# Delta layer with the value folded into the reduce, one fold on GpSimd and eight taps on TensorE, keys moved from SBUF to SBUF, and full-height chunks in the expert layer

## What is computed

```
h = einsum('bsd,ehd->bseh', xn, w_up);  val, gate = split(h, 2)
h = val * silu(gate)                       # 704 hidden values
y = einsum('bseh,edh->bsed', h, w_down)    # 704 -> 256
```

```
q = silu(x @ Wq);  k = silu(x @ Wk);  k = k * rsqrt(sum(k*k) + 1e-12);  v = x @ Wv
beta = 2*sigmoid(x @ Wbet);  a = sigmoid(x @ Wf)
def step(S, inp):
    qt, kt, vt, at, bt = inp
    Sd = at * S
    u  = vt - einsum('bhk,bhkv->bhv', kt, Sd)
    Sn = Sd + bt * kt[..., None] * u[:, :, None, :]
    o  = einsum('bhk,bhkv->bhv', qt, Sn)
    return Sn, o
o = o * rsqrt(mean(o*o) + 1e-6) * norm_w;  return o @ Wo
```

## Time and profile before

| | us |
|---|---|
| median of 3 runs (lowest, highest) | 1418.88 (1416.88, 1424.58) |
| the profiled execution's own time | 1413.77 |
| its span in the trace | 1412.1 |
| TensorE, busy in the span | 1141.6 (81%) |
| VectorE, busy | 826.9 (59%) |
| ScalarE / GpSimd, busy | 564.8 (40%) / 565.7 (40%) |
| mean granted TensorE clock | 0.915 of full speed |

### The profile page before, as it was taken

How to read it: one execution, slowest core, us unless ns; L and a number is a source line. 1 busy time by engine, 2 the same in 40 slices (tenths; PEclk the granted TensorE clock), 3 DMA queues, 4 the chain that set the end, 5 groups by cost and what they waited for, 6 DMA issues and landing times. The chain is left out here.

```text
span 1412.1 us, 23993 instructions
## 1 busy us (share of the span) xinstructions
PE 1141.6 (81%) x8723; PEld 841.3 (60%) x8723; DVE 826.9 (59%) x1978; ACT 564.8 (40%) x1340; POOL 565.7 (40%) x626
## 2 busy tenths in 40 slices
PE   6999984898999999686667777774699999867854
PEld 4666662787889889532234444433577777645533
DVE  3666666211211211456999999997477777532886
ACT  2544552111111112155565666663234444325544
POOL 0111111232333233243699999995122222120657
PEclk9999995899999999799898999997799999979885
DMA  4111100988888887387000000001100040026601
GB/s 134 43 46 46 35 13 13 355 341 319 308 308 316 302 316 267 98 219 191 0 0 1 0 1 0 1 0 59 28 9 13 9 153 36 2 76 255 205 19 57
DMA packets 83349, 162.19 MB, mean 115 GB/s; under 512 B 44128, under 2 KB 62176, under 8 KB 77216
## 3 DMA queue, kind: packets, MB, share of 16 engines
q1 hardware_dynamic: 55536, 111.23, 23.0%
q0 software_dynamic: 10512, 45.10, 8.7%
q10 hardware_dynamic: 17184, 4.33, 1.4%
HBM read 134.28 MB, written 26.35 MB: 114 GB/s over the span
## 5 line engine op out<-in xcount | busy, mean ns | idle before, releaser
L1419 PE MATMUL banks<-made,ident 128*128 128x512 f32 x256 | 152.3, 680 | 91.2 <-DVE made L1630 90.6
L920 PE MATMUL banks<-rowsT,w_up 128*128 128x128 f32 x1716 | 201.3, 278 | 0.0
L920 PEld LDWEIGHTS banks<-rowsT,w_up 128*128 128x128 f32 x1716 | 198.0, 195 | 0.5 <-issue 0.3
L1682 POOL TENSOR_TENSOR ys<-xT_d,q_by_time 128x1024 f32<-128x1024 f32 x63 | 148.6, 2359 | 19.7 <-ACT xT_d L1502 9.8
L1525 ACT ACTIVATE banks<-banks,rate 128x256 f32<-128x256 f32 x256 | 103.9, 444 | 117.7 <-DVE made L1621 117.7
L1419 PEld LDWEIGHTS banks<-made,ident 128*128 128x128 f32 x256 | 41.5, 203 | 155.5 <-ACT banks L1525 130.3
L1686 POOL TENSOR_TENSOR ys<-ys 128x512 f32<-128x512 f32 x126 | 124.8, 990 | 9.9
L935 PE MATMUL banks<-w_down,hT 128*128 128x256 f32 x468 | 115.1, 388 | 0.6 <-DVE res L1100 0.6
L1090 DVE TENSOR_TENSOR hT<-banks,silu 64x128 f32<-64x128 f32 x39 | 11.0, 282 | 171.4 <-ACT silu L978 171.4
L864 POOL DMA_DIRECT2D w_down<-in_down_w x39 | 22.7, 583 | 199.8 <-PE banks L935 191.2
L935 PEld LDWEIGHTS banks<-w_down,hT 128*128 128x128 f32 x468 | 82.6, 189 | 22.0 <-issue 13.9
(11 more groups left out here) (312 smaller groups left out, 2305.8 us busy)
## 6 DMA issues: line engine op xcount, KB each, us to landing
w_up<-in_up_w SPq DMA_DIRECT2D x39, 1408.0 KB, 6.0
w_down<-in_down_w POOLq DMA_DIRECT2D x39, 768.0 KB, 5.6
inter<-res_x SPq DMA_DIRECT2D x16, 512.0 KB, 3.3
back<-inter SPq DMA_DIRECT2D x15, 512.0 KB, 3.9
patches<-in_patches SPq DMA_DIRECT2D x16, 384.0 KB, 3.3
f<-in_f SPq DMA_DIRECT2D x6, 1024.0 KB, 11.5
ys<-token_rows SPq DMA_DIRECT2D x16, 256.0 KB, 2.9
xn_rows<-xn_all SPq DMA_DIRECT2D x16, 128.0 KB, 1.7
```

What stands on the lines that cost most here:

```text
L920: ins = pe.matmul(out[:, m * P:(m + 1) * P], w[:, c, m * P:(m + 1) * P], x[:, c, :], start=(c == 0), stop=(c == 1))
L1419: pe.matmul(S[(t + 1) % 2][:, halves[h], :, :], ident[:, :], outer[:, halves[h], :, :], start=False, stop=True, skip_group_check=True).the ...
L1682: pool.tensor_tensor(qs[:, :, :, :], Sc[(t + 1) % 2][:, :, :, :], bcast(qt[:, t, :, :], 2, HD), ALU.mult).then_inc(sem("qs_made"), 1)
```

## The change

Four edits.

1. Experts: the sixth product of `down` takes all 128 rows. GpSimd zeroes the lower 64 rows of that chunk in both `hT` buffers once (the weights are padded in DRAM already), and TensorE waits for that once.
2. Recurrence, VectorE: `ka` is made with a minus sign, `prod` has 17 elements a value instead of 16, and the 17th is v. So one reduce of 544 elements gives u, and L1627 goes. The 17th element is written by ScalarE (`place_values`), for token t+1 between the fades and `copy_out`, and it waits for u of token t.
3. Recurrence, GpSimd and TensorE: one fold (16 to 8) instead of two, and eight slices in `sum_folded` instead of four, four of them after each half's `add_outer`.
4. Front: the keys go from `made` to `chain_k` straight, in 16 DMAs a group of 16 x 8 x 64 elements (32 KB); no DRAM. The columns of Wk are reordered for it on the host's side of the weights, so that a piece holds 16 heads x 8 dimensions.

```diff
@@ expert_layer
+        for p in range(2):
+            pool.memset(hT[p][HLAST:P, FULL, :], 0.0).then_inc(sem("h_padded"), 1)
...
             for c in range(HIDC):
-                n = P if c < FULL else HLAST
-                ins = pe.matmul(Y, hT[j % 2][0:n, c, :], w_down[j % DEEP][0:n, c, :], start=(c == 0),
-                                stop=(c == FULL))
+                ins = pe.matmul(Y, hT[j % 2][:, c, :], w_down[j % DEEP][:, c, :], start=(c == 0), stop=(c == FULL))
...
+        pe.wait_ge(sem("h_padded"), 2)
@@ delta_layer, SyncE
         def send_keys(g):
-            store_made(sp, g, 2)
-            store_made(sp, g, 3)
+            for m in (2, 3):
+                sp.wait_ge(sem(f"made{m}"), g + 1)
+                for b in range(8):
+                    lanes, dims = slice(b * HEADS, (b + 1) * HEADS), slice(m % 2 * 8, m % 2 * 8 + 8)
+                    sp.dma_start(k[lanes, g, dims, :], made[m][:, b * TOK:(b + 1) * TOK]
+                                 ).then_inc(sem(f"stored{m}"), 16)
...
-            load_chain(sp, g, "k", k)
@@ TensorE
-        def sum_folded(t):
-            pe.wait_ge(sem("qs_folded"), 2 * t + 2)
-            if t:
-                pe.wait_ge(sem("o_made"), t)
-            for n in range(4):
-                ins = pe.matmul(o_sum, ident[:, :], products[t % 2][:, :, :, n], start=(n == 0), stop=(n == 3))
-            ins.then_inc(sem("o_folded"), 1)
+        def sum_folded(t, h):
+            if h == 0:
+                pe.wait_ge(sem("qs_folded"), t + 1)
+                if t:
+                    pe.wait_ge(sem("o_made"), t)
+            for n in range(FOLDED // 2 * h, FOLDED // 2 * (h + 1)):
+                ins = pe.matmul(o_sum, ident[:, :], products[t % 2][:, :, :, n], start=(n == 0),
+                                stop=(n == FOLDED - 1))
+            if h:
+                ins.then_inc(sem("o_folded"), 1)
...
-            add_outer(t)
-            if t >= 2:
-                sum_folded(t - 2)
+            for h in range(2):
+                add_outer(t, h)
+                if t >= 2:
+                    sum_folded(t - 2, h)
@@ ScalarE
+        def place_values(t, h):
+            return act.copy(prod[:, halves[h], :, HD], v[:, halves[h], :, t])
...
+                if t + 1 < TOK:
+                    act.wait_ge(sem(f"u_made{h}"), t + 1)
+                    ins = place_values(t + 1, h)
                 ins.then_inc(sem(f"faded{h}"), 1)
@@ VectorE
-                dve.tensor_tensor(prod[:, at, :, :], S[t % 2][:, at, :, :], bcast(ka[:, t, at, :], 2, HD),
+                dve.tensor_tensor(prod[:, at, :, 0:HD], S[t % 2][:, at, :, :], bcast(ka[:, t, at, :], 2, HD),
                                   ALU.mult).then_inc(sem(f"prod_made{h}"), 1)
                 dve.wait_ge(sem(f"prod_made{h}"), t + 1)
-                dve.tensor_reduce(read[:, at, :], prod[:, at, :, :], AX.X, ALU.add
-                                  ).then_inc(sem(f"read_made{h}"), 1)
-                dve.wait_ge(sem(f"read_made{h}"), t + 1)
-                dve.tensor_tensor(u[:, at, :], v[:, at, :, now].rearrange("p g d o -> p g (d o)"),
-                                  read[:, at, :], ALU.subtract).then_inc(sem(f"u_made{h}"), 1)
+                dve.tensor_reduce(u[:, at, :], prod[:, at, :, :], AX.X, ALU.add).then_inc(sem(f"u_made{h}"), 1)
@@ GpSimd
-            for i, n in enumerate((8, 4)):
-                pool.tensor_tensor(qs[:, :, :, 0:n], qs[:, :, :, 0:n], qs[:, :, :, n:2 * n],
-                                   ALU.add).then_inc(sem("qs_folded"), 1)
-                pool.wait_ge(sem("qs_folded"), 2 * t + i + 1)
+            pool.tensor_tensor(qs[:, :, :, 0:FOLDED], qs[:, :, :, 0:FOLDED], qs[:, :, :, FOLDED:2 * FOLDED],
+                               ALU.add).then_inc(sem("qs_folded"), 1)
```

More of the change, by code:

```diff
@@ L1284, in delta_layer @@
     Sc = [by_state(xT[i][:, :, :].rearrange(states)) for i in range(2)]
-    prod, outer = (by_state(made_all[:, 2 * i:2 * i + 2, :].rearrange(states)) for i in range(2))
+    flat = made_all[:, :, :].rearrange(states)
+    n_prod, n_outer = CG * HD * (HD + 1), CG * HD * HD
+    prod = flat[:, 0:n_prod].rearrange("p (g v k) -> p g v k", g=CG, v=HD)
+    outer = by_state(flat[:, n_prod:n_prod + n_outer])
     squares = w[:, :, :].rearrange("p c n -> p (c n)")[:, 0:HD * CG * CUTS[1]].rearrange("p (d n) -> p d n", d=HD)
-    last_squares = made_all[:, 4:6, :].rearrange(states)[:, 0:CG * HD * LAST].rearrange("p (g d t) -> p g d t", g=CG, t=LAST)
+    last_squares = flat[:, n_prod + n_outer:n_prod + n_outer + CG * HD * LAST].rearrange("p (g d t) -> p g d t", g=CG, t=LAST)
     products = [by_state(front["ys"][:, 2 * i:2 * i + 2, :, :].rearrange("p n k d -> p (n k d)")) for i in range(2)]
@@ L1294, in delta_layer @@
     o_sum = banks[:, 5, 0:CG * HD].rearrange("p (g v) -> p g v", g=CG)
-    small = banks[:, 4, :].rearrange("p (n g v) -> p n g v", g=CG, v=HD)
-    read, u = small[:, 0, :, :], small[:, 1, :, :]
+    u = banks[:, 4, 0:CG * HD].rearrange("p (g v) -> p g v", g=CG)
     halves = [slice(2 * h, 2 * h + 2) for h in range(2)]
@@ L1457, in tensor @@
                     sum_squares(n, t - CUTS[n + 1] - 6)
-        sum_folded(TOK - 2)
+        for h in range(2):
+            sum_folded(TOK - 2, h)
     def scalar(act):
@@ L1477, in step @@
                     if g:
[L1478 removed]
+                        act.wait_ge(sem(f"stored{m}"), (128 if m in (2, 3) else 16) * g)
                     act.activation(made[m][:, :], banks[:, 2 + m, :], func).then_inc(sem(f"made{m}"), 1)
@@ L1491, in square_keys @@
         def square_keys(g):
-            act.wait_ge(sem(f"chain_k{g}"), 16)
+            for m in (2, 3):
+                act.wait_ge(sem(f"stored{m}"), 128 * g + 128)
             act.square(o[:, g, :, :], k[:, g, :, :]).then_inc(sem("k_squared"), 1)
@@ L1518, in scalar @@
         act.preload_act_table_set("natural_log_exp_and_others")
+        for g in range(CG):
+            act.wait_ge(sem(f"chain_v{g}"), 16)
+        for m in range(6):
+            act.wait_ge(sem(f"stored{m}"), (128 if m in (2, 3) else 16) * CG)
+        for h in range(2):
+            place_values(0, h).then_inc(sem("values_placed"), 1)
         for t in range(TOK):
@@ L1610, in vector @@
         for m in range(6):
-            dve.wait_ge(sem(f"stored{m}"), 16 * CG)
+            dve.wait_ge(sem(f"stored{m}"), (128 if m in (2, 3) else 16) * CG)
         dve.wait_ge(sem("kb_made"), CG)
         dve.wait_ge(sem("q_turned"), CG)
-        for g in range(CG):
-            dve.wait_ge(sem(f"chain_v{g}"), 16)
+        dve.wait_ge(sem("values_placed"), 2)
         for t in range(TOK):
-            now = slice(t, t + 1)
             for h in range(2):
@@ L2628, in laid_out_more @@
         "tile_no": line(np.arange(SLOTS)),
-        "delta_w": rows(np.concatenate([a("L1_attn_Wq"), a("L1_attn_Wk"), a("L1_attn_Wv")], 1)),
+        "delta_w": rows(np.concatenate([a("L1_attn_Wq"), a("L1_attn_Wk").reshape(D, HEADS, 2, HD // 2).transpose(0, 2, 1, 3).reshape(D, D),
+                                       a("L1_attn_Wv")], 1)),
         "rate_w": rows(np.concatenate([a("L1_attn_Wbet"), a("L1_attn_Wf")], 1)),
```

20 lines of the change are left out of this document (10 added, 10 removed).

## The result

| us | before | after |
|---|---|---|
| median of 9 runs each (lowest, highest) | 1421.86 (1414.55, 1427.48) | 1411.61 (1408.44, 1417.96) |
| the profiled execution's own time | 1413.77 | 1409.07 |
| its span | 1412.1 | 1407.4 |
| mean granted TensorE clock | 0.915 | 0.921 |

What follows compares the result with a forecast made beforehand. It took TensorE to bound the experts and VectorE the recurrence, with GpSimd a close second. Experts -12, recurrence -6.5 and keys +1 made -17.5 us, so 1401 us from a median of 1418.9, range 1388 to 1413.

Steps and rivals of the forecast that it cites:

- a recurrence that gives back what it gains: Rival, recurrence: dearer `place_values` slot or clock falls as before, step 4.6, total -6, 1413 us; chance 0.20.
- 16 issues 0.4 to 0.5 apart: Sign of a right forecast, front: SyncE's sixteen key issues stand 0.4 to 0.5 us apart.
- Keys: +1: Front: sixteen issues on SyncE delay the rates, not the keys, costing ScalarE and the front 1 us; ends 0 and 4.
- late rates decide the front: Rival, front: each piece holds SyncE 0.95 us, sixteen take 15, a tanh comes some 8 later, 1409 us; chance 0.05.
- The last group's squares at 660.17 are set by ScalarE's order, so earlier keys bring nothing: Front: the last group's keys are squared without idle time ahead, so no gain was counted for earlier keys.
- Full-height chunk, -12: Experts: TensorE saves 0.35 us a tile at the sixth product of `down`, 12 us in all.
- The wait on `o_made`: Recurrence: slices ahead of the second half's `add_outer` wait for ScalarE's `store_out`, making the step 4.50 us.
- the part on VectorE: Recurrence: without L1627 and with a longer reduce, a step is 4.18 us if VectorE decides, 0.42 less.
- the recurrence's -6.5: Recurrence in sum: -6.3 for the step, +1 given up in early steps, +4 squares, -3.2 clock.
- Sums of squares, +4: Recurrence: TensorE has little room left in steps with squares, 1.4 us a chunk, 4 in all.
- Clock, -3: Recurrence: TensorE idles less, so its falls to half clock go, saving 3.2 us.
- Slower at half clock: Rival, recurrence: TensorE at half clock makes a step 7.0 us; 15 such steps give 1438; chance 0.07.

Runs made afterwards that it cites:

- a_double_made: Changed kernel with the rates' two stores ahead of the key pieces and a second pair of buffers for keys as made: 1411.74 us, ratio 0.9945.
- a_pool_pieces: Changed kernel with eight of the sixteen key pieces issued from GpSimd's queue, ahead of its `kb`: 1407.5 us, ratio 0.9911.
- b_pad_only: Kernel before with the full-height chunk of the experts alone: 1406.1 us, ratio 0.9930.
- b_rec_only: Kernel before with the recurrence's edits alone (17th element, one fold, slices between the halves): 1412.03 us, ratio 0.9958.
- a_pool_slices_last: Changed kernel with eight key pieces from GpSimd's queue and all eight slices behind both halves of `add_outer`: 1390.04 us, ratio 0.9788.
- a_best_spread: Changed kernel with keys through DRAM, all slices behind both halves of `add_outer`, and sums of squares in smaller parts: 1377.46 us, ratio 0.9717.

## Why the prediction was wrong

The sign was right, the size was not: half of the 17.5 us is missing, 0.6% came for 1.3%, and one term does most of it. That 1411.6 lies within the range (up to 1413) is luck: its upper end stood for a recurrence that gives back what it gains, step 4.6 and more, and the recurrence didn't; the front did. The prediction's own sign, "16 issues 0.4 to 0.5 apart", failed: they stand 0.6 apart at the least, mostly 0.64.

- **The step that failed: "Keys: +1".** It priced an issue at 0.42 to 0.57 us, from two stores, 7 to 9 for sixteen, and said "This delays not the keys ... but what stands behind them in SyncE's queue: the rates". Measured: 0.64 us for most and 0.69 to 0.77 on average, 11.0 to 12.4 us for sixteen, and then 2.0 to 5.6 until the last has landed. And it is the keys that are late. Two things wait for the last piece, and I had costed neither: ScalarE's next `made` (7.72 us idle), and the squares. That `stored` semaphores guard `made` for the next group was in the kernel text; with two stores of 0.4 us they were never late. a_double_made takes the first wait away and keeps the second, a_pool_pieces takes the second away and keeps the first. The first then idles TensorE, and at half clock eight products take another 2 us in the second cycle. Together +12.6 by the trace, +10.6 by the medians with and without the edit (+16 made alone, interval 11 to 22, 3 of them in the loop). Why the last piece lands after 2.0 us in one group and 5.6 in another stays open.
- **The rival "late rates decide the front"** (0.05) put sixteen issues at 15 us, measured 11.0 to 12.4, and the loss at 8, but through the rates. They were not what ScalarE waited for.
- **The sentence from the Trainium skill**, DMA: Bandwidth & Descriptors (Measured, under Bandwidth), gives 0.95 us for 64 KB, the time in the DMA engines of a load from HBM; 15 us for the row of pieces was an estimate from it. The traces have 11.0 to 12.4 us, of issues. My sum went by a row of two issues and had 7 to 9; the one was about as far too high as the other was too low.
- **"The last group's squares at 660.17 are set by ScalarE's order, so earlier keys bring nothing"** was true of the kernel before. I used it for earlier keys and didn't ask it of later ones: in the kernel after they wait 2.70 us.
- **Full-height chunk, -12: right.** 0.35 a tile as forecast, 13.6 in all; 2.4 of it in the one tile that waits for gathered rows, which took from 9.7 to 12.7 in the traces here, whatever the kernel. b_pad_only: -0.70%, 9.9 us.
- **The wait on `o_made`: right**, mechanism and place, and shown twice (moved, and uncoupled): without it the step is 4.17, as the part on VectorE had it (4.18). Its size was 4.50 and is 4.56: the slot of `place_values` 0.15 where I took 0.10 between 0 and 0.28, and the slices 0.94 where I took 0.87, less 0.07 in the other links. Over some 50 steps 0.06 is 3 us, which is what the recurrence's -6.5 lacks in the trace. (b_rec_only has -6.0 by the medians.)
- **Sums of squares, +4**: (5.55 + 4.62 + 4.89 + 4.18) - 4 x 4.56 = 1.0 a chunk, +3. Right in kind.
- **Clock, -3**: right. Of six falls in the loop one is left (at 684.6, with one step of 5.31), and b_pad_only has eight while b_rec_only has none.
- **Slower at half clock** did not come in the changed kernel's loop. Its price, a step of 7.0, was about right: a_pool_slices_last has one of 7.43 at half clock.
- **The chances** have a slip: "a third of giving back" is 0.07 of the 0.20, and the sum uses 0.11.

With the failed term at its measured size the sum is -12 - 6.5 + 12.6 = -5.9, and -4.7 is what the two spans differ by.

## What to carry to other kernels

Count a DMA cut into pieces by its issues (here 0.64 to 0.77 us each on SyncE, for 16 KB as for 32), add the landing of the last (2.0 to 5.6 us), and then ask who waits for the last piece: the reader of the target, and also the writer of the source. A trip through DRAM with three issues beat sixteen that save the trip. When a change brings a wait on a single buffer ahead of work that others need, a second buffer or three lines of order may be worth more than the change: here 20 us of the loop, against the 3 to 4 that the whole edit of the recurrence had brought.

## What was not expected of the hardware

- An issue of 16 KB took as long as one of 32 KB: 0.66 us against 0.64 on SyncE, undisturbed. One of 32 KB took 0.65 on ScalarE (5.22 / 8) and 0.53 on GpSimd (4.24 / 8). Some issues took much longer, up to 1.7 us on SyncE. The second store of q on ScalarE's queue took 1.46 us in the third cycle of the changed kernel, in place of 0.4; but with no pieces at all a_best_spread has one of 1.30 there, so this is not the pieces' doing alone.
- An idle time of TensorE of 4.8 to 5.7 us was followed by half clock for part of the next eight products, 5.65 and 6.12 us for 3.60, and one of 2.37 us too (5.40). One of 2.31 us in the kernel before, at 613.5, was not. So a DMA wait of one engine is paid again on another.
- In the loop, TensorE idled 1.54 us of each step of 4.60 and its clock fell six times; now it idles 0.8 to 1.2 of 4.56, in one place instead of two, and one fall is left.
